# A transformer layer with routed experts on one core: the first expert blocks from five batches, their table inside iteration 6, block 0 inside iteration 7

## What is computed

```python
x = x + attention(layernorm(x), ctx, ctx, mask)     # 16 heads of depth 16, masked softmax, @ Wo + bo
xf = layernorm(x).reshape(N, d)
scores = softmax(xf @ w_gate)                       # 8 experts
weights, idx = top_k(scores, 2)                     # pos: place of the token in its expert, capacity 1024
a, g = split(exp_x @ c_fc)                          # per expert, 256 -> 2 x 384
exp_out = (silu(a) * g) @ c_proj                    # 384 -> 256
out = x + sum over the two experts of exp_out[expert, pos] * weight
```

## Time and profile before

| what | value |
|---|---|
| three runs, us | 433.62, 431.9, 434.6; median 433.62 |
| the profiled execution, us | 432.8 |
| its span (first to last instruction), us | 430.7 |
| its mean granted TensorE clock | 0.950 of full |
| PE busy | 370.0 us (86%) |
| VectorE busy | 248.4 us (58%) |
| ScalarE busy | 214.0 us (50%) |
| GpSimd busy | 165.7 us (38%) |

### The profile page before, as it was taken

The page is one execution under the profiler, slowest core; times in us unless marked ns, Lnnn a source line. Parts: engine busy times, 40 slices in busy tenths (PEclk is TensorE's granted clock), DMA queues, the critical chain, the costliest instruction groups (busy, mean ns, idle before and its releaser), DMA issues.

```text
span 430.7 us, 9281 instructions
## 1 busy us (share of the span) xinstructions
PE 370.0 (86%) x2752; PEld 292.7 (68%) x2753; DVE 248.4 (58%) x693; ACT 214.0 (50%) x342; POOL 165.7 (38%) x174
## 2 busy tenths in 40 slices
PE   5437895898899999998988599989899999999990
PEld 3324663565566656665654399878699999999980
DVE  4636656589988988887878356752233332333320
ACT  2620474557466665744446568534244454544440
POOL 5020152342747658241253005742233334243332
PEclk9956699899999999999999699999899999999997
DMA  6589259387784949487136213554432332424330
GB/s 201 123 197 191 53 178 187 132 187 198 162 201 173 202 166 206 131 187 190 50 137 215 82 50 62 130 107 87 73 62 46 62 48 47 73 42 73 51 56 4
DMA packets 65468, 51.93 MB, mean 121 GB/s; under 512 B 11898, under 2 KB 62346, under 8 KB 65418
## 3 DMA queue, kind: packets, MB, share of 16 engines
q1 hardware_dynamic: 58028, 42.71, 40.6%
q0 software_dynamic: 7008, 8.43, 12.0%
q10 hardware_dynamic: 400, 0.40, 0.3%
HBM read 32.89 MB, written 19.06 MB: 121 GB/s over the span
## 4 chain that ended last, share of the span: by engine, by line
PE 55%; DMA 18%; DVE 9%; issue 7%; SPq 6%; ACT 3%; POOL 1%; POOLq 0%; ACTq 0%; DVEq 0%
PE bank L1032 19%; PE bank L1043 9%; DMA out<-CTt,GG 7%; PE bank L987 5%; DVE NEG L1170 5%; PE bank L875 5%; PE bank L958 4%; PE bank L919 3%; PE bank L892 3%; DMA wf<-NMT 3%; DMA wf<-qparts_d 3%; PE bank L971 3%; PE bank L883 2%; DMA slots<-R,slot 2%; PE bank L1012 2%
## 5 line engine op out<-in xcount | busy, mean ns | idle before, releaser
L1032 PEld LDWEIGHTS bank<-CX,KS 128*128 128x128 f32 x912 | 109.0, 194 | 6.4 <-issue 4.7
L1032 PE MATMUL bank<-CX,KS 128*128 128x128 f32 x912 | 109.9, 278 | 2.4 <-issue 2.3
L1170 DVE TENSOR_REDUCE NEG<-bank 128x2 f32<-128x512 f32 x128 | 85.7, 685 | 35.7 <-PE bank L958 34.3
L761 ACT ACTIVATE PR<-bank 128x512 f32<-128x512 f32 x128 | 73.2, 591 | 47.2 <-PE bank L971 46.5
L665 POOL DMA_INDIRECT out<-CTt,GG x38 | 58.9, 1549 | 97.6 <-DMA out<-CTt,GG 60.8
L801 ACT ACTIVATE KS<-wf 128x1536 f32 x40 | 59.2, 1483 | 43.1 <-PE bank L1032 42.6
L1398 DVE COPY CX<-bank 128x256 f32<-128x256 f32 x39 | 16.5, 424 | 77.2 <-PE bank L1012 77.2
L958 PE MATMUL bank<-KS,wf 99*128 99x256 bf16 x224 | 45.6, 290 | 15.9 <-DMA wf<-qparts_d 10.2
L1043 PE MATMUL bank<-wp,QF 128*128 x228 | 56.9, 386 | 2.4 <-DVE CTt L1412 2.4
L584 POOL DMA_INDIRECT slots<-R,slot x32 | 32.7, 1022 | 38.0 <-DVE slot L1276 26.5
L971 PE MATMUL bank<-wf,KS 102*128 102x256 bf16 x224 | 43.2, 273 | 3.9 <-DMA wf<-NMT 3.2
(11 more groups left out here) (171 smaller groups left out, 466.4 us busy)
## 6 DMA issues: line engine op xcount, KB each, us to landing
wf<-in_L_ffn_c_fc SPq DMA_DIRECT2D x8, 768.0 KB, 5.2
XG<-slots SPq DMA_DIRECT2D x40, 128.0 KB
kparts_d<-KP SPq DMA_DIRECT2D x8, 384.0 KB, 2.5
KS<-kparts_d SPq DMA_DIRECT2D x8, 384.0 KB
KS<-kparts_d SPq DMA_DIRECT2D x24, 128.0 KB
qparts_d<-QP SPq DMA_DIRECT2D x8, 384.0 KB, 3.1
wp<-in_L_ffn_c_proj SPq DMA_DIRECT2D x8, 384.0 KB, 4.9
wf<-qparts_d SPq DMA_DIRECT2D x7, 384.0 KB
```

The source lines that it names most:

```text
L761: act.activation(PR[:, s % NPROB, :], STB[s % 2][:], ACT.Exp).then_inc(exp_done, 1)
L1032: ins = pe.matmul(bank[2 + 2 * u + g][:, c * P:(c + 1) * P], UP[u][:, (k * 2 + g) * FF + c * P:(k * 2 + g) * FF + (c + 1) * P], XTG[:, u, ...
L1170: dve.tensor_reduce(NEG[:, n % 2, t, 2 * hp:2 * hp + 2], MXB[m % 2][:].rearrange("p (i s) -> p i s", i=2), AX.X, ALU.max, negate=True).the ...
```

## The change

- `KNOWN` is 5: the first twelve blocks come from batches 0 to 4. CNT(5) is made at unit 1 of iteration 6, and `ahead_table` is cut in four: `ahead_full`, `ahead_taken`, `blocks_experts`, `blocks_table`, at units 1, 4, 6 and 11 of iteration 6. The table of the rest is cut in two (`rest_experts`, `rest_table`), a block apart.
- PE turns the rows of blocks 0 and 1 at units 1 and 3 of iteration 7 and does block 0's up-projection at units 10 and 13, in banks 1 and 0. ACT copies block 0's weights at unit 8. From block 1 the hidden banks are 4 - 2u and 5 - 2u.
- SP loads blocks 0 and 1 ahead of the last expert weights and of batch 7's second max rows. GG has four places, so the gates of blocks 0 to 3 are loaded at once and those of 4 to 10 wait for the add four before; the pads stand at blocks 8, 9 and 10 (3, 3, 2).
- From block 5 on, blocks of odd number have a down bank of their own (MISC[0]).
- POOL adds blocks 0, 1, 2, scatters batch 6, adds block 3, scatters batch 7.
- The order around blocks 0 to 5 is changed on PE, ACT and DVE.

```diff
-KNOWN = B - 2
+KNOWN = B - 3
...
+    "counts": 1, "first full": 1, "first taken": 4, "first experts": 6, "first table": 11,
+    "rows 0": 1, "rows 1": 3, "up 0": 8, "hidden a": 10, "hidden g": 13,
...
-LAST_MISC = {0: [("PF", B - 3)], 1: [("NM1", B - 1)], 3: [("CNT", KNOWN)], 6: [("WO", B - 2)]}
-TAIL_MISC = [("X2", B - 2), ("WO", B - 1), ("LG", B - 2), ("PF", B - 2), ("X2", B - 1),
+LAST_MISC = {0: [("PF", B - 3)], 1: [("NM1", B - 1)], 6: [("WO", B - 2)]}
+GATES = 4
+TAIL_MISC = [("X2", B - 2), ("WO", B - 1), ("LG", B - 2), ("X2", B - 1), ("PF", B - 2),
...
+    if (it, unit) == (B - 2, AT["counts"]):
+        pieces.append(("CNT", KNOWN))
...
+def gate_place(t, u):
+
+    return t % GATES if not later(t, PEELED - 1) else u
+
+
+def two_banks(t):
+
+    return later(t, 5)
...
+        def down_bank(t, u):
+            return MISC[0] if u == 1 and two_banks(t) else bank[1]
+
+        def hidden_bank(t, u, g):
+            return bank[4 - 2 * u + g] if later(t, 1) else bank[1 - g]
...
-                if later(t, 2):
+                if later(t, PEELED - 1):
                     sp.wait_ge(added[u], (t - u) * 8)
...
+                elif later(t, GATES):
+                    sp.wait_ge(added[u], (t - GATES - u) * 8 + 16)
...
-            max_rows(B - 1, 1)
-            load_weights(B - 1)
             sp.wait_ge(ahead_ready, 1)
...
             load_block(0, 0)
             load_block(1, 1)
-            load_gates(0, 0)
-            load_gates(1, 1)
-            store_rows(B - 2)
+            load_weights(B - 1)
+            max_rows(B - 1, 1)
+            for t in range(GATES):
+                load_gates(t, t % 2)
...
-            for t in range(7, AHEAD):
+            padded = {8: range(0, 3), 9: range(3, 6), 10: range(6, E)}
+            for t in range(4, AHEAD):
                 load_block(t, t % 2)
-                load_gates(t - 3, (t - 3) % 2)
-                if t == AHEAD - 4:
+                if t > GATES:
+                    load_gates(t - 1, (t - 1) % 2)
+                if t == 8:
                     sp.wait_ge(pad_at_ready, 1)
...
-            for t in range(2):
+            for t in range(3):
                 add_block(t, t % 2)
             scatter(B - 2)
-            for t in range(2, 4):
-                add_block(t, t % 2)
+            add_block(3, 1)
             scatter(B - 1)
...
+                if u == AT["up 0"]:
+                    act.wait_ge(ahead_ready, 1)
+                    act.wait_ge(we_in, 32 * E)
+                    copy_up(0, 0)
             copy_up(1, 1)
             silu(0, 0)
+            copy_up(2, 0)
             evacuate("X2", B - 2)
             copy_rows(B - 2)
-            copy_up(2, 0)
             silu(1, 1)
             copy_up(3, 1)
-            router_exponentials(B - 2)
             silu(2, 0)
+            copy_up(4, 0)
             evacuate("X2", B - 1)
             copy_rows(B - 1)
-            copy_up(4, 0)
+            router_exponentials(B - 2)
             silu(3, 1)
...
+                    if it == B - 1 and u == AT["rows 0"]:
+                        pe.wait_ge(mx_reduced, UNITS * B)
+                        turn_rows(0, 0)
+                    if it == B - 1 and u == AT["rows 1"]:
+                        turn_rows(1, 1)
+                    if it == B - 1 and u == AT["hidden a"]:
+                        pe.wait_ge(up_ready, 1)
+                        pe.wait_ge(txe_ready, 2)
+                        hidden_half(0, 0, 0)
+                    if it == B - 1 and u == AT["hidden g"]:
+                        hidden_half(0, 0, 1)
...
+                    if u == AT["first full"] and it == B - 2:
+                        ahead_full()
+                    if u == AT["first taken"] and it == B - 2:
+                        ahead_taken()
+                    if u == AT["first experts"] and it == B - 2:
+                        blocks_experts(taken_incl[:], taken[:, 0:E], AHEAD)
+                    if u == AT["first table"] and it == B - 2:
+                        blocks_table(0, AHEAD, None, ahead_ready)
...
+            split_max(B - 1, 1)
             rows_copy(0, 0)
+            route_gates(B - 3)
+            route_slots(B - 3)
+            rows_copy(1, 1)
+            normalize_product(B - 2, 1)
+            turn_product(B - 2)
+            residual(B - 2)
+            stats2_of(B - 2)
+            normalize_product(B - 1, 0)
             normalize2(B - 2)
             normalize_product(B - 1, 1)
             turn_product(B - 1)
-            rows_copy(1, 1)
             gated(0, 0)
+            rows_copy(2, 0)
+            gated(1, 1)
             residual(B - 1)
             stats2_of(B - 1)
...
+            weigh(0, 0)
             normalize2(B - 1)
...
             weigh(1, 1)
+            rows_copy(4, 0)
+            gated(3, 1)
             route_gates(B - 2)
             route_slots(B - 2)
...
             step(5, 1)
+            rest_experts()
+            step(6, 0)
             rest_table()
-            step(6, 0)
+            step(7, 1)
             rest_pairs()
```

More of the change, by code:

```diff
@@ L785, in _ @@
                         router_exponentials(it - 1)
-            for u in range(UNITS):
-                exponentials(B - 1, u)
-                for kind, n in misc_at(B - 1, u):
-                    if kind == "NM1":
-                        evacuate(kind, n)
             up_at = act.alloc_register("up_at")
@@ L990, in values, with turn_rows, at, load_down_at @@
                 ins.then_inc(av_done, 1)
+            def turn_rows(t, u):
+                pe.wait_ge(xg_in[u], (t - u) * 8 + 16)
+                if later(t, 1):
+                    pe.wait_ge(txe_ready, t)
+                if later(t, 2):
+                    pe.wait_ge(hm_ready, 1)
+                for k in range(KC):
+                    ins = pe.transpose(bank[0][:, k * P:(k + 1) * P], XG[:, u, k * P:(k + 1) * P], ident[:])
+                ins.then_inc(tx_ready, 1)
+            down_at = [pe.alloc_register("down_at0"), pe.alloc_register("down_at1")]
+            def at(register, largest):
+                return pe.snap(register, min_val=0, max_val=largest)
+            def load_down_at(t, u):
+                pe.reg_load(down_at[u], table[0:1, 2, bass.ds(t, 1)])
+            def hidden_half(t, u, g):
+                for c in range(FC):
+                    for k in range(KC):
+                        ins = pe.matmul(hidden_bank(t, u, g)[:, c * P:(c + 1) * P],
+                                        UP[u][:, (k * 2 + g) * FF + c * P:(k * 2 + g) * FF + (c + 1) * P], XTG[:, u, k, :],
+                                        start=k == 0, stop=k == KC - 1)
+                ins.then_inc(h_ready if g else ha_ready, 1)
+            def hidden(t, u):
+                pe.wait_ge(up_ready, t + 1)
+                pe.wait_ge(txe_ready, t + 1)
+                if later(t, 2):
+                    pe.wait_ge(hm_ready, t - 1)
+                for g in range(2):
+                    hidden_half(t, u, g)
+            def down(t, u):
+                off = at(down_at[u], (E - 1) * FC * D)
+                pe.wait_ge(hm_ready, t + 1)
+                if two_banks(t):
+                    pe.wait_ge(ys_ready, t - 1)
+                elif later(t, 1):
+                    pe.wait_ge(ys_ready, t)
+                for c in range(FC):
+                    ins = pe.matmul(down_bank(t, u)[:, 0:D], HM[:, u, c * P:(c + 1) * P], wp[:, bass.ds(off + c * D, D)],
+                                    start=c == 0, stop=c == FC - 1)
+                ins.then_inc(y_ready, 1)
+            def step(t, u):
+                hidden(t, u)
+                turn_rows(t + 1, 1 - u)
+                down(t - 1, 1 - u)
+                load_down_at(t, u)
             pe.wait_ge(const_step, CONST_IDENT)
@@ L1037, in down @@
-            def down(t, u):
-                off = at(down_at[u], (E - 1) * FC * D)
-                pe.wait_ge(hm_ready, t + 1)
-                if later(t, 1):
-                    pe.wait_ge(ys_ready, t)
-                for c in range(FC):
-                    ins = pe.matmul(bank[1][:, 0:D], HM[:, u, c * P:(c + 1) * P], wp[:, bass.ds(off + c * D, D)],
-                                    start=c == 0, stop=c == FC - 1)
-                ins.then_inc(y_ready, 1)
-            def step(t, u):
-                hidden(t, u)
-                turn_rows(t + 1, 1 - u)
-                down(t - 1, 1 - u)
-                load_down_at(t, u)
```

106 lines of the change are left out of this document (31 added, 75 removed).

## The result

The changed kernel took 438.24 us (median), the kernel before on the same chip 434.77 us: ratio 1.0069, 95% interval 1.004 to 1.010. It is slower by 0.7%, inside the 1% that was called no change, and above both the forecast (429.1) and its range (423.5 to 436.5). The profiled execution took 435.39 us, its span is 433.5 us. Ratios leave out executions of a second, slower state that any of these kernels falls into at times, and medians in us leave out none, so the two need not divide exactly.

The account below looks back on a forecast made before the run. The prediction took PE to bound the expert-block loop, so block 13's start sets the end; gains of 0.2 us up to block 9 and 4.3 from there to block 13 sum to 4.5, giving 429.1 us, range 423.5 to 436.5.

Parts of the forecast that it names:

- Which view and what bounds it: The expert-block loop is bound by PE at 4.19 us per block, so the end moves with block 13's start.
- Iteration 6, +2.0: The table's four pieces on VectorE lengthen iteration 6 by 2.0 us, with bounds of 0.5 and 5.0.
- Unit 11 stands beside the unread projections on PE, which need nothing of VectorE: nothing sticks: Iteration 6: the table's last piece, 1.65 us on VectorE, adds nothing at unit 11.
- Iteration 7 to block 2, -4.2: Logits end at 245.5 us, then 9.2 us at full clock, so block 2 starts at 254.7, 2.2 earlier.
- The gain booked for taking block 0 away from behind the iteration: Behind iteration 7, idle time, slow clock and block 0 gone are 9.7 us; 7.5 is spent before.
- Blocks 2 to 9, the adds: GpSimd's adds, 7.8 us apart around scatters, decide: add 4 at 284.4, block 9 at 290.3, gain shrunk to 0.2 us.
- Blocks 9 to 13, 17.7: Weighing no longer waits for late gates; four blocks take 17.7 us against 22.0, a gain of 4.3.
- Adds take it all back: Rival, chance 0.22: slow landings at adds 4 and 5 put 2.4 us on the path, giving 431.5 us.
- the half clock in iteration 7: Rival, chance 0.11: PE's wait at WO(6) grows, the rest of iteration 7 runs at 1.2 GHz, costing 8.8 us: 437.9.
- Hidden table: Rival, chance 0.22: iteration 6 swallows the table's pieces and rows land before PE asks, giving 424.4 us.
- The sum: Whole kernel up to block 13: 0.2 plus 4.3 make 4.5 us of gain, forecast 429.1 us.

Follow-up runs that it names:

- a0_after: The changed kernel, unedited, run and profiled again on another occasion: 437.08 us, ratio 1.0111 to the kernel before.
- e1_bias: The changed kernel with GpSimd's two bias additions held back until the first blocks' table is ready: 433.55 us, ratio 1.0042.
- e6_up0: The changed kernel with GpSimd's bias addition waiting for the table and block 0's up-projection behind iteration 7 instead of inside it: 435.27 us, ratio 1.0083.
- e2_scatter: The changed kernel with GpSimd's old order, two adds instead of three ahead of batch 6's scatter: 436.73 us, ratio 1.0107.
- e5_three: The changed kernel with three edits: bias addition waits for the table, two adds ahead of batch 6's scatter, SyncE's stores moved: 429.69 us, ratio 0.9963.
- e8_two_places: The changed kernel with table wait, two adds before batch 6's scatter and stores moved, but two gate places as before: 434.33 us, ratio 1.0000.
- e9_gates: The kernel before with only four gate places and the changed kernel's SyncE order, run in more rounds: 431.05 us, ratio 0.9933.
- e12_gates: The kernel before with only four gate places and the changed kernel's SyncE order, on a third chip: 432.57 us, ratio 0.9925.
- e13_two: The same kernel as e8_two_places, run again on one more chip: 434.94 us, ratio 0.9978.
- e3_gates: The kernel before with only four gate places and the changed kernel's SyncE order, first run: 430.15 us, ratio 0.9961.

## Why the prediction was wrong

**Which view and what bounds it: right.** The end moved with block 13, the loop kept 4.19 us per block, and the idle time behind iteration 7 and the stall at the loop's entry went, with the clock at 1.00 from 233.8 us on (in a0_after and e1_bias it still fell to half once, behind block 10's wait).

**Iteration 6, +2.0: right in size, one price wrong.** Without the collision it is 25.8 to 26.1 us at full clock, in four profiles, against 24.2 and twice 23.5 with the table where it was: 1.6 to 2.6. The failed step is "Unit 11 stands beside the unread projections on PE, which need nothing of VectorE: nothing sticks". It looked at the engine that waits for VectorE and not at the one that works beside it. The durations came from the earlier trace rows, read where GpSimd did no arithmetic; at unit 11 it adds the bias. That is 2.7 us on the instruction, 0.9 of it in iteration 6 and 1.2 behind it. The trace of before held the sign: VectorE's AVN<-AVT,RSUM takes 1.21 us or more wherever GpSimd multiplies or adds whole tiles beside it and 0.43 elsewhere, which I didn't look for.

**Iteration 7 to block 2, -4.2: right but for the collision.** 29.0 was foretold, 29.4 came without the collision and 30.6 with it. That block 0's rows were in time and WO(6) late was the collision's doing too: PE reached the rows later, and VectorE reached the product later. Without it (e1_bias) the rows kept PE 0.73 us and WO(6) stood at 9.6 us, as foretold. The clock did not stay at 1.00 up to block 9 in either, but the half clock cost at most the 0.4 us that e1_bias took over the forecast. The gain booked for taking block 0 away from behind the iteration was already spent within it: 0.2 us net (e6_up0). And block 2's start flattered the change: PE's work from block 2 to 9 rose by 8 matmuls (250 for 242, 1.3 us more busy in a0_after), since LG(6) now comes behind block 2's up-projection. That is part of the 1.9 us by which blocks 2 to 9 were foretold to grow, for which I had named the adds alone.

**Blocks 2 to 9, the adds: mechanism right.** The 7.8 us spacing was exact, and e2_scatter shows that the adds set block 9. The foretold length was 35.6 us, the runs with this order gave 36.0, 36.2, 36.0 and 36.9; the changed kernel's 37.4 holds a standstill of its own. Add 4 was late because everything ahead was.

**Blocks 9 to 13, 17.7: the step that failed most.** It came out at 20.2, 21.6 and 21.6. "SyncE sends three pads before block 10's load (0.75 each), so PE waits 0.9": a pad takes 1.1 to 1.3 us (0.75 was half the 1.47 us that two of them show in the trace of before, where the next issue came 2.3 us behind the first); the wait came out at 2.25 and 2.82. Three pads and block 10's rows stand behind gates 8, which wait for add 4's landing, and block 9's rows stand behind the three pads before. I took gates in four places as free of the adds; they are free of the add two blocks back, not of the one four back, and that is the late one. With the adds and stores put right (e5_three) it is 18.3, as with the gates alone.

**Rivals.** "Adds take it all back" (431.5) came nearest in mechanism: no change that can be told, from late adds with pads and loads queued behind them, though by the adds' start and not by slow landings. In number the half clock in iteration 7 (437.9) came nearest, by luck: the clock did fall, but ahead of PF(5)'s wait and not at WO(6), for 6.8 us of light work and not for the rest of the iteration; e1_bias had the same and came within 0.4 us of the forecast's 29.0, where 8.8 were named. "Hidden table" is refuted.

**The sum** was 4.5 us of gain. Over the stages to block 13 the repairs bring 5.1 (e5_three). So by the stages the change could do what was booked, but only with GpSimd and SyncE put in order around it, and by the times it then gives no more than the gates' places alone.

**Open.** The single profile of before (430.7 us, 24.2 in iteration 6) doesn't convert into times to better than some 2 us: e5_three's stages say 1.2%, its runs 0.4 to 0.5%. And one kernel's ratio moved from 0.992 to 1.001 between chips for no reason that I found.

## What to carry to other kernels

Before work is moved into a gap of one engine, read what every other engine does at that time: the cost was set not by who waits for VectorE but by what GpSimd computed beside it. When an in-order queue has a wait in it, list all that stands behind the wait, and put in front what doesn't need it; a wait that moved from two blocks back to four is still a wait. And try the parts of a change alone: the smallest of them, four places for gates and their loads, carried what gain was measured (0.4 to 0.75%), and beside the large one it could not be seen.

## What the runs showed of the hardware

VectorE instructions with two inputs in SBUF were held up beside GpSimd's arithmetic on whole SBUF tiles. Here VectorE's timeline of the changed kernel in iteration 5, then GpSimd's:

```profile
181.79 0.25 DVE L1218 RECIPROCAL RSUM<-AVT 128x16 f32<-128x16 f32 x1
182.07 1.21 DVE L1219 TENSOR_TENSOR AVN<-AVT,RSUM 128x256 f32<-128x256 f32 x1
183.32 0.69 DVE L1197 TENSOR_REDUCE NEG<-bank 128x2 f32<-128x512 f32 x1
183.93 0.70 DVE L1225 STREAM_TRANSPOSE ON<-AVN 128x512 f32<-128x512 f32 x1
```
```profile
181.85 1.16 POOL L346 TENSOR_TENSOR KP<-KREST,KP 128x512 bf16<-128x512 f32 x1 [0.44 <-ACT KP L758]
182.96 1.34 POOL L346 TENSOR_TENSOR QP<-QREST,QP 128x512 bf16<-128x512 f32 x1
```

The two-input multiplication (0.43 us alone) ends at 183.28, 0.27 us behind the end of GpSimd's first operation (183.01): it began about when that one ended, and GpSimd's next then took 1.34 us in place of 1.16. The reduction (its input in PSUM) and the transpose, with one input, keep their times beside it. Beside GpSimd's smallest operation (128x2) a two-input operation (128x16) kept its time too, 0.17 us at 192.07 in the same trace. At unit 11 the operation of 0.17 us waited out both additions, 2.90 us. By the Trainium skill, "SBUF — State Buffer", section "Who interferes with whom", a VectorE instruction with two SBUF inputs contends with a GpSimd instruction that reads SBUF, and whichever comes second blocks in full. The traces agree that VectorE waits, and e1_bias shows it by its removal. Who comes second they don't settle: at unit 11 VectorE's record starts 0.32 us ahead of GpSimd's first addition, and it waited all the same.

In the traces of the changed kernel, e8_two_places, e9_gates, e12_gates and e13_two, several engines stand still at once for 2 us and more, once or twice between blocks 4 and 9; the profile names no releaser, or one outside the core ("issue", "remote"). PE in e9_gates and then VectorE in e12_gates:

```profile
271.61 0.57 PE L1036 MATMUL bank<-CX,KS 128*128 128x128 f32 x3 [2.28 <-issue]
```
```profile
274.80 0.42 DVE L1402 COPY CX<-bank 128x256 f32<-128x256 f32 x1 [5.41 <-remote]
```

These traces hold 6,350 to 6,430 semaphore records; the other eight in the table, without such a standstill, hold 7,200 to 7,220. e3_gates, e9_gates and e12_gates are one kernel: 32.5 us for blocks 2 to 9 without, 38.8 and 37.4 with it, and then 18.3 against 16.8 twice, which fits adds that catch up meanwhile. The Trainium skill, "NOTIFIC — the notification-queue block", section "Overflow: three behaviours, one of which stalls the engine", knows both of a full record queue, records dropped and an engine stalled; no run here shows that it is the cause, nor whether executions without a profile have these standstills. A length that takes in blocks 2 to 13 therefore compares only between traces of one kind.
